# Attention mask, layer norms and a top-2 mixture of eight experts: VectorE's work ahead of the first expert, the place of the gate's picks, and the order of TensorE's last scores and constant products

## The reference

```python
sim = einsum('bhnd,bhmd->bnm', Q, K) / (sqrt(16) * 4)      # Q, K = ctx @ Wq.T, ctx @ Wk.T
k = int(256 * 0.3)                                          # 76
A = sigmoid(sim) * (sim >= top_k(sim, k)[0][:, :, -1:])
A = (A + swapaxes(A, -1, -2)) * 0.5
x = x + (1 - gamma) * layernorm(x) + gamma * A              # gamma = sigmoid(gamma_raw)
...
probs = softmax(layernorm(x) @ gate_w)
gate_score, gate_idx = top_k(probs, 2)                      # scaled to sum 1
combine = (gate_score with one_hot(gate_idx)) * alpha
h = gelu(einsum('th,ehi->eti', xn, fc1_w) + fc1_b)
y = einsum('eti,eih->eth', h, fc2_w) + fc2_b
x = x + einsum('eth,te->th', y, combine)
```

## Time and profile before

| | us |
|---|---|
| median of 3 runs | 130.49 (130.37 to 130.55) |
| the profiled execution, its own time | 130.1 |
| its span, first to last instruction | 128.3 |
| PE busy in the span | 119.2 |
| DVE, ACT, POOL busy | 96.2, 87.6, 65.0 |

### The profile page before, as it was taken

The page is one execution under the profiler, slowest core; times in us unless marked ns, Lnnn a source line. Parts: engine busy times, 40 slices in busy tenths (PEclk is TensorE's granted clock), DMA queues, the critical chain, the costliest instruction groups (busy, mean ns, idle before and its releaser), DMA issues.

```text
span 128.3 us, 2763 instructions
## 1 busy us (share of the span) xinstructions
PE 119.2 (93%) x904; PEld 108.6 (85%) x904; DVE 96.2 (75%) x399; ACT 87.6 (68%) x212; POOL 65.0 (51%) x66
## 2 busy tenths in 40 slices
PE   6796989899969999999999999999999999999990
PEld 3443656699949999999899999998999999999990
DVE  0068989886987898999979999999787337823481
ACT  3178999899999979454897784729646544555510
POOL 2039668638647944643097456512972545444400
PEclk9999999999999999999999999999999999999999
DMA  2999999952996000002000000200000002000002
GB/s 66 198 390 415 405 321 174 192 101 29 181 169 119 5 0 3 0 5 82 3 0 0 3 8 0 81 1 8 0 0 0 5 0 82 0 5 0 3 0 82
DMA packets 3380, 10.05 MB, mean 78 GB/s; under 512 B 396, under 2 KB 868, under 8 KB 3364
## 3 DMA queue, kind: packets, MB, share of 16 engines
q1 hardware_dynamic: 2500, 6.71, 14.7%
q0 software_dynamic: 864, 3.15, 14.3%
HBM read 8.81 MB, written 1.05 MB: 77 GB/s over the span
## 4 chain that ended last, share of the span: by engine, by line
PE 41%; DVE 36%; ACT 13%; issue 6%; POOL 1%; DVEq 0%; POOLq 0%; ACTq 0%
PE p_y L477 17%; PE p_h L455 16%; DVE acc L1061 8%; ACT h_act L579 3%; ACT w_lo L564 2%; ACT w_hi L557 2%; DVE top L886 2%; DVE above L842 2%; DVE stats L745 2%; ACT h_hi L587 2%; PE p_y L355 2%; DVE left L891 1%; DVE picked L1018 1%; ACT act_waste L543 1%; DVE best_f L1004 1%
## 5 line engine op out<-in xcount | busy, mean ns | idle before, releaser
L698 POOL TENSOR_TENSOR h_lo<-h_act,h_hi 128x512 fp32r<-128x512 f32 x31 | 40.2, 1300 | 45.4 <-ACT h_hi L587 32.6
L579 ACT ACTIVATE h_act<-p_h,small_sb 128x256 f32<-128x256 f32 x64 | 26.6, 467 | 19.4 <-PE p_h L455 19.3
L455 PE MATMUL p_h<-xt_hi,w_hi 128*128 128x256 f32 x128 | 32.9, 280 | 1.1 <-ACT h_act L579 1.0
L455 PE MATMUL p_h<-xt_hi,w_lo 128*128 128x256 f32 x128 | 32.6, 278 | 0.0
L1061 DVE SCALAR_TENSOR_TENSOR acc<-p_y,comb,acc 128x256 f32<-128x256 f32 x55 | 24.0, 475 | 11.0 <-PE p_y L477 10.2
L477 PE MATMUL p_y<-w_hi,h_hi 128*128 128x256 f32 x126 | 26.0, 288 | 1.0 <-DVE acc L1061 1.0
L455 PEld LDWEIGHTS p_h<-xt_hi,w_hi 128*128 128x128 f32 x128 | 24.1, 188 | 1.6 <-issue 1.5
L455 PE MATMUL p_h<-xt_lo,w_hi 128*128 128x256 f32 x128 | 25.3, 279 | 0.0
L477 PE MATMUL p_y<-w_lo,h_hi 128*128 128x256 f32 x126 | 24.9, 279 | 0.0
L477 PE MATMUL p_y<-w_hi,h_lo 128*128 128x256 f32 x126 | 24.9, 279 | 0.0
L455 PEld LDWEIGHTS p_h<-xt_hi,w_lo 128*128 128x128 f32 x128 | 24.1, 188 | 0.0
(11 more groups left out here) (141 smaller groups left out, 191.1 us busy)
## 6 DMA issues: line engine op xcount, KB each, us to landing
w_sb<-w SPq DMA_DIRECT2D x8, 512.0 KB, 8.3
w_lo<-w POOLq DMA_DIRECT2D x6, 512.0 KB, 5.6
x_sb<-x SPq DMA_DIRECT2D x1, 768.0 KB, 8.5
out<-acc SPq DMA_DIRECT2D x3, 256.0 KB, 2.5
x_sb<-x SPq DMA_DIRECT2D x1, 256.0 KB, 4.4
out<-acc SPq DMA_DIRECT2D x2, 128.0 KB, 2.0
attn_sb<-attn SPq DMA_DIRECT2D x1, 192.0 KB, 5.1
small_sb<-small SPq DMA_DIRECT2D x1, 97.5 KB, 4.7
```

Of the source, the lines that this page charges most:

```text
L455: last = nc.tensor.matmul(dst, w_[:, e, 0, k, c * P:(c + 1) * P], v[:, b % 2, k, :], start=n == 0, stop=n == len(trio) - 1)
L579: last = nc.scalar.activation(h_act[:, s % 2, c], tiled(p_h[s % 2])[:, c, :], ACT.Gelu, bias=b1_sb[:, e, c:c + 1])
L698: nc.gpsimd.tensor_tensor(h_lo[:, s % (LAG + 1)], h_act[:, s % 2], h_hi[:, s % (LAG + 1)], ALU.subtract).then_inc(h_lo_ready, 1)
```

## The change

It has six parts. (1) `gamma_terms` stands at DVE's start instead of in the chain of batch 0; for it SP loads small_sb ahead of the rest of attn, and ACT takes gamma's tanh right after `u_copy(0)`. (2) `flag_few` and `flag_missed` are one instruction over both tiles each instead of one per tile, and `missed_ready` counts one for a batch. In batch 0 `better_guess` is taken apart. (3) `ln1_affine(0)` goes from DVE to POOL, `ln1(1)` from DVE's front to step 1 of the loop. (4) The gate's picks and weights are written to free columns of the PSUM bank p_g, the sum of two picks is a reduction there, and the cast of the two places is one instruction for each number. (5) PE makes the scores of batch 3 behind the masked transposes instead of ahead of them, the constant products behind it are 5 instead of 18, and 5 instead of 3 behind xn's transposes. (6) POOL rounds experts 0, 2, 1, 6 and 7 instead of 0, 1 and 2, and ACT's and POOL's early lists are reordered to fit.

```diff
-POOL_HI = 3
+POOL_HI = (0, 2, 1, 6, 7)
+ACT_HI = (3, 4, 5)
+POOL_HI_AT = {0: 6, 2: 7}
-WARM_BEFORE_XN = 18
+WARM_BEFORE_XN = 5
...
+        PICKED = p_g[:, at:at + TILES * 2 * EXPERTS].rearrange("p (t j e) -> p t j e", t=TILES, j=2)
+        WEIGHT = p_g[:, at:at + TILES * EXPERTS].rearrange("p (t e) -> p t e", t=TILES)
...
             sp.dma_start(x_sb[:, 0], x[:, 0:TILES]).then_inc(x_in[0], 16)
+            sp.dma_start(small_sb[:], small).then_inc(small_in, 16)
             sp.dma_start(attn_sb[:, first:], attn[:, first:]).then_inc(ctx_in, 16)
-            sp.dma_start(small_sb[:], small).then_inc(small_in, 16)
...
@@ the DVE helpers @@
-                for t in range(TILES):
-                    dve.wait_ge(counted, b * TILES + t + 1)
-                    nc.vector.tensor_scalar(few[:, t:t + 1], count[:, t:t + 1], TOP_K - WINDOW, None,
-                                            ALU.is_lt).then_inc(few_ready, 1)
+                dve.wait_ge(counted, (b + 1) * TILES)
+                nc.vector.tensor_scalar(few[:], count[:], TOP_K - WINDOW, None, ALU.is_lt).then_inc(few_ready, 1)
...
-                step(nc.vector.tensor_copy(best_f[:], best_at[:, :, 0:2]))
+                for t in range(TILES):
+                    for r in range(2):
+                        step(nc.vector.tensor_copy(best_f[:, t, r:r + 1], best_at[:, t, r:r + 1]))
...
-                        step(nc.vector.tensor_scalar(picked[:, t, r], iota_sb, best_f[:, t, r:r + 1],
+                        step(nc.vector.tensor_scalar(PICKED[:, t, r], iota_sb, best_f[:, t, r:r + 1],
                                                      score[:, t, r:r + 1], ALU.is_equal, ALU.mult))
                 settle()
-                step(nc.vector.tensor_tensor(weight[:], picked[:, :, 0], picked[:, :, 1], ALU.add))
+                step(nc.vector.tensor_reduce(WEIGHT, PICKED.rearrange("p t j e -> p t e j"), AX.X, ALU.add))
...
@@ POOL ahead of the loop @@
             weight_lo(0, 0)
-            weight_hi(1)
-            weight_hi(2)
+            ln1_affine(0)
             base(0)
-            weight_lo(1, 0)
-            weight_rest(2)
             pool.wait_ge(gate_hi_ready, 1)
             nc.gpsimd.tensor_tensor(gate_parts[:, :, 1], gate_sb, gate_parts[:, :, 0], ALU.subtract).then_inc(
                 gate_lo_ready, 1)
+            weight_hi(2)
+            pool.wait_ge(base_sum, 1)
+            weight_hi(1)
+            rstd(veps2, rstd2, 0, ln2_veps, ln2_rstd)
+            pool.wait_ge(xn_ready, TILES)
+            weight_rest(2)
+            weight_lo(1, 0)
+            weight_lo(0, 1)
             weight_rest(3)
-            pool.wait_ge(masked, TILES)
-            weight_lo(0, 1)
-            rstd(veps2, rstd2, 0, ln2_veps, ln2_rstd)
-            weight_rest(4)
-            pool.wait_ge(xn_ready, TILES)
             weight_lo(1, 1)
```

More of the change, by code:

```diff
@@ L169, in xattn_moe_program @@
         score = sb("score", [P, TILES, 2])
-        picked = sb("picked", [P, TILES, 2, EXPERTS])
-        weight = sb("weight", [P, TILES, EXPERTS])
         comb = sb("comb", [P, BATCHES, TILES, PARTS, EXPERTS])
@@ L370, in similarities @@
                 sum_missed(0)
-                for b in range(2, BATCHES):
-                    sim_of(b)
+                sim_of(2)
             def transpose_masked(b):
@@ L604, in _ @@
             u_copy(0)
+            act.wait_ge(small_in, 16)
+            nc.scalar.activation(gam[:, 0:1], gamma_sb, ACT.Tanh, scale=0.5).then_inc(gam_th, 1)
             sim_copy(0)
@@ L608, in _ @@
             signs_again_of(0)
-            act.wait_ge(small_in, 16)
-            nc.scalar.activation(gam[:, 0:1], gamma_sb, ACT.Tanh, scale=0.5).then_inc(gam_th, 1)
             for b in range(1, BATCHES):
                 u_copy(b)
+            nc.scalar.activation(gate_parts[:, :, 0], gate_sb, ACT.Copy).then_inc(gate_hi_ready, 1)
             sigmoid(0)
+            weight_hi(3)
+            sim_copy(1)
+            spread_of(1)
             weight_neg(2)
-            weight_hi(3)
             weight_neg(3)
-            for b in range(1, BATCHES):
-                sim_copy(b)
-            nc.scalar.activation(gate_parts[:, :, 0], gate_sb, ACT.Copy).then_inc(gate_hi_ready, 1)
-            spread_of(1)
+            sim_copy(2)
             weight_hi(4)
-            weight_neg(4)
+            sim_copy(3)
             signs_of(1)
@@ L649, in _ @@
                     sigmoid(b + 1)
-                    base(b + 1)
+                    if b:
+                        base(b + 1)
+                if s == 3:
+                    base(1)
                 if e == 5:
@@ L686, in base, with ln1_affine @@
                 last.then_inc(base_ready, 1)
+            def ln1_affine(b):
+                pool.wait_ge(gam_ready, 1)
+                pool.wait_ge(ln1_agg, (b + 1) * TILES)
+                pool.wait_ge(ln1_rstd, b + 1)
+                for t in range(TILES):
+                    nc.gpsimd.tensor_scalar(mul1[:, b, t:t + 1], rstd1[:, b, t:t + 1], gam[:, 2:3], ones[:], ALU.mult,
+                                            ALU.add)
+                    last = nc.gpsimd.tensor_scalar(add1[:, b, t:t + 1], mv1[:, b, t, 0:1], gam[:, 3:4],
+                                                   rstd1[:, b, t:t + 1], ALU.mult, ALU.mult)
+                last.then_inc(ln1_mul, 1)
             def add_masked(b):
@@ L838, in better_guess @@
                                         ALU.subtract).then_inc(better_ready, 1)
+            def better_guess(b, t):
+                offset_again(b, t)
+                second_guess(b, t)
             def count_above(b, t):
@@ L855, in flag_missed @@
                     dve.wait_ge(missed_sum, b)
-                for t in range(TILES):
-                    dve.wait_ge(few_ready, b * TILES + t + 1)
-                    nc.vector.tensor_scalar(missed[:, t:t + 1], count[:, t:t + 1], TOP_K, few[:, t:t + 1],
-                                            ALU.is_ge, ALU.add).then_inc(missed_ready, 1)
+                dve.wait_ge(few_ready, b + 1)
+                nc.vector.scalar_tensor_tensor(missed[:], count[:], TOP_K, few[:], ALU.is_ge,
+                                               ALU.add).then_inc(missed_ready, 1)
             steps = [0]
@@ L1086, in _ @@
                 middle_guess(0, t)
-            for t in range(TILES):
-                better_guess(0, t)
-                count_above(0, t)
-            flag_few(0)
-            gamma_terms()
+            offset_again(0, 0)
+            second_guess(0, 0)
+            offset_again(0, 1)
+            count_above(0, 0)
+            second_guess(0, 1)
+            count_above(0, 1)
             drop_above(0)
-            ln1_affine(0)
             take_eight(0)
@@ L1101, in _ @@
             add_masked(0)
-            ln1(1)
             residual(0)
@@ L1125, in _ @@
                 if s == 1:
+                    ln1(1)
                     combine(0)
```

43 lines of the change are left out of this document (26 added, 17 removed).

## The result

The changed kernel takes 134.29 us (133.91 to 134.63), the one before 130.43 us (130.14 to 130.55) in runs beside it: a ratio of 1.029, 95% interval 1.027 to 1.031. The forecast of 128.8 is 5.5 us off and the sign is wrong. The profiled execution has a span of 132.8 us, 4.5 more than before.

A forecast was written before the change was run, and what follows sets the result against it. PE was taken as the bound past step 5, so its start and stalls move the end one for one. 0.9 us at step 5 plus 0.8 in the gates, 1.7 off 130.49, gave 128.8 us; range 127.7 to 130.3.

The forecast's parts named there:

- The front: DVE's chain up to xn: 1.2 us saved up to the first search, residual 2.0 earlier, xn 1.8 earlier.
- bound of 0 to 0.5: Front: delay of ACT's first score copy by gamma's tanh waiting for small_sb; taken as 0, with 0.5 the other end.
- The 0.2 that was set aside for POOL: Front: two-column flags with both operands in SBUF may wait for POOL; 0.2 us taken of a possible 0 to 0.6.
- POOL behind xn: POOL's weight work after xn takes 10.6 us; expert 5's DMA issues at 32.1, lands at 37.7, and up(5) waits for it.
- step 5: Expert loop at up(5): start moves from 38.60 to 37.7, a gain of 0.9 us.
- The gates: Batches 1 and 2: flags, casts and picks save 0.46 us in batch 1; both 0.43 stalls go, 0.8 counted together.
- POOL's chain stretches: Rival, chance 0.13: POOL's ten links from xn to expert 5's DMA take 0.2 us more each beside DVE; 130.8 us.
- The sentence that named the waiting step down(8): Reading of PE's timeline: PE is full from up(5) until 62.26, where down(8) waits for DVE's acc.
- Cold PE: Rival, chance 0.12: first experts run at 1.2 GHz, step 5 gains 0.4 instead of 0.9; 129.3 us.
- the prediction's own sign of 0.21: Sign that the forecast is wrong: up(0) to up(2) have 0.21 us between products.
- Picks no cheaper in PSUM: Rival, chance 0.12: gate picks cost no less in PSUM, the stalls stay in good part, gain 1.0; 129.5 us.
- Landings do bind: Answers a rival, chance 0.12: weight landings don't bind, POOL's chain is 1.2 us shorter, step 5 gains 2.1; 127.6 us.

The follow-up runs named there:

- e14: Changed kernel with POOL waiting for batch 1's flags ahead of its last split of expert 1, and 192 unused bytes kept allocated ahead of comb: 128.68 us, ratio 0.9872.
- e1: Changed kernel with one wait added: POOL holds its last split of expert 1 until DVE has flagged batch 1; 130.17 us, ratio 0.9985.
- e11: Changed kernel with only the 192 bytes of two unused SBUF tiles kept allocated ahead of comb: 132.80 us.

## Why the prediction was wrong

- **The front**: right. 1.83 us earlier at xn against 1.8. From the better guess to the first search DVE took 3.81 before (from 10.57) and 2.50 now (from 10.84), 1.31 less for the 1.2 counted. But it began 0.27 later, as ACT's first score copy starts 0.3 later, behind gamma's tanh, inside the bound of 0 to 0.5; the search itself is 1.04 earlier. `residual` came 1.82 earlier (18.10) for the 2.0 counted. The 0.2 that was set aside for POOL was not taken by POOL (`few` 0.19, `missed` 0.15) but by this later start, so that the agreement is partly luck.
- **POOL behind xn**: right where DVE is not kept out. In e14 expert 5's DMA goes out at 32.17 (32.1) and takes 5.8 us to land (5.6), and up(5), which waits for it, starts at 38.04 (37.7). So step 5 gains 0.56 and not 0.9.
- **The step that failed, first: DVE beside POOL.** The prediction let work with two SBUF inputs lose "0.2 of the possible 0 to 0.6", from casts that ended with the running POOL instruction, and for the front alone. It wrote down that POOL's list behind xn is one row without a gap, 10.6 us, and that DVE is busy beside it, but gave the loss a price on POOL's side only (the rival of stretched links, 0.2 each). What it had wrong is that the wait is not bounded by the POOL instruction that runs: the pass was passed over through five of them, 6.55 us for 0.41. POOL's list left no pause from 21.80 to 31.96, and it ended only where POOL itself waited for DVE. 4.12 us (e1).
- **The step that failed, second: two tiles removed at no cost.** The picks in PSUM were priced as instructions alone; that their tiles free 192 bytes and move h_hi and h_lo was put at nothing, without a reason. 1.49 us (e11).
- **The gates**: right in the sum, not in its terms, and hidden by the second cost. Without it batches 1 and 2 take 24.51 and 24.56 in e14 against 25.04 and 25.06 before, 1.03 us for the 0.8 that was counted, as a stall cost 0.52 and not 0.43. From `few` to the acc of expert 8 DVE takes 7.76 in e14 and 8.21 before, 0.45 for the 0.46 counted; but the flags gave 0.29 (0.2 counted), the casts 0.17 (0.16) and the picks 0.01 (0.1), so that this too is partly luck. In the changed kernel `few` was held beside POOL, and the same stretch took 8.34: longer than before. No stall followed, since `few` came 0.84 earlier after up(8), and PE, with its wider distances, came later to down(10). The sentence that named the waiting step down(8) was wrong: the stalls of the earlier trace rows are at down(10) and down(18), which wait for the add of experts 8 and 16.
- **The total of e14**: 0.1 from the forecast, with 0.34 too little at step 5 and 0.23 too much in the gates. The mechanisms hold; that it comes so near is partly luck.
- **The rivals**: "POOL's chain stretches" had the sign and the place, and a wrong mechanism. POOL's chain was not stretched (from its first DMA to that of expert 5, 10.49 in e14 for the 10.6 counted; in the changed kernel 10.16 up to its wait, for 9.9), and the 4 us are one wait. "Cold PE" came true for up(0), as the prediction's own sign of 0.21 shows: it ran at 0.213 between most products in the changed kernel and in e1, and near 0.12 in e14. It cost little, as up(5) starts at 38.09 in e1 and 38.04 in e14, held by the landing in both. "Picks no cheaper in PSUM" was right about the picks (0.86 for 0.87) and wrong about the stalls, which went all the same. Landings do bind: in e14 PE waits for them three times, 2.2 us in all.

## What to carry to other kernels

Before moving POOL work into one row, list the DVE instructions beside it that read two SBUF tiles; each can be held over several of POOL's instructions, and if POOL's next pause is a wait for DVE the loss can be the whole row. One PSUM input, a pointer operand, or a wait placed in POOL's list avoids it. When a stall goes and the time stays, compare the distance between PE's products before looking for a new wait, and when tiles are removed, keep the addresses behind them until both have been timed.
